# A fused attention and feed-forward kernel: in the first pair of blocks, flags, small products, weight loads and one operand's rounding are placed anew

## The chip, the core and the metric

The kernel runs on one core of one Trainium2 chip. The metric is the device time of one execution in microseconds (us), the median of several runs. TensorE (PE in the profile) does the matrix products, VectorE (DVE) and ScalarE (ACT) work between PSUM and SBUF, GpSimd (POOL) works on SBUF alone here, and SyncE (SP) issues nearly all DMA transfers. The engines run their own instruction streams in order and wait for each other on semaphores.

## What is computed

Linear attention without a softmax, a layer norm, a gated feed-forward part with two hidden layers, and a second layer norm, over 4096 tokens of 256 features. The weights of the feed-forward part are ternary numbers (times 8) with a scale for each output.

```python
def attn(x, wq, wk, wv, wo):                    # x (1, 4096, 256), D = 64
    Q, K, V = x @ wq.T, x @ wk.T, x @ wv.T
    energy = einsum('bnd,bne->bde', K, V)
    context = einsum('bnd,bde->bne', Q, energy) * sqrt(3 / D)
    return context @ wo.T

def ffn(x, w1, s1, w2, s2, h1, t1, h2, t2, w3, s3):   # 256 -> 1024 -> 1024 -> 1024 -> 256
    lin = lambda x, w, s: (x @ w.T) * s
    h = silu(lin(x, w1, s1)) * lin(x, w2, s2)
    h = gelu(lin(h, h1, t1))
    h = gelu(lin(h, h2, t2))
    return lin(h, w3, s3)

x = layernorm(x + attn(x, ...))
x = layernorm(x + ffn(x, ...))
```

## The kernel before

**Tiles.** The tokens are eight blocks of 512, worked on as four pairs (p = 0 to 3). Activations stand feature by token. Each fp32 activation that TensorE multiplies is given in two fp32r parts: ScalarE rounds it (`hi`, L674), VectorE subtracts (`lo`, L944), and both parts are multiplied with the same weights.

**Hidden layers.** Each of the two 1024x1024 layers of a pair is done by Winograd's form of the 2x2 product: seven products of 512x512 weights with 512x512 activations. I write product l.n for product n of hidden layer l (of the first pair, if nothing else is said). A product is four tiles j of eight matmuls (L1322), 32 in all, into four PSUM banks. GpSimd makes the differences of the activations (L506, L516, L525, L528), ScalarE copies sums out of PSUM (`copy_out`, L690) and applies the gelu (L720), VectorE adds (`add_first` L951, `add_fourth` L957, `add_third` L963). `R` has three slots, so product n uses slot n mod 3; the weights come through a ring of three slots as well (`load_ring`, L333).

**The first pair is special.** Its weights arrive in it. Eight units of the hidden weights (`unit`, 1 MB each) are loaded, GpSimd makes their sums in place (`combine`, L446 to L452), they are stored to a DRAM tensor `combos`, and the ring is loaded from there; two of the seven weight sets need no sums and are copied from DRAM to DRAM (`relay_hidden`). Blocks 2 to 7 load their residual rows late, since the upper halves of their places in `xr` hold `beside4` and `beside5`, a part of the sums.

**Flags and looks.** The products may take the rounded weights only if the low bits of all weights are zero. ScalarE sums the low bits as the weights arrive (`bits`, L569), TensorE adds these over the partitions (`flag_sum(s)`, L1211), VectorE makes a number 0 or 1 of it (`flag_out(s)`, L866 and L868), and TensorE reads it into a register and branches (`load_flag(s)`, L1217 and L1230). There are seven such looks; what follows look s in TensorE's stream can't start before the branch. Look 1 stands ahead of the first gated layer `first_l1` (L1262), look 2 ahead of product 0.0, look 3 ahead of 0.2, look 4 ahead of 1.0, look 5 ahead of 1.2.

**Order.** Everything is in an order written by hand, in loops for each engine: `first_l1`, `hidden`, and the list of transfers on SyncE. In `first_l1` ScalarE makes a silu (L640) and VectorE a gated product (`gate`, L938) for each of 8 chunks of two blocks (beta 0, 1); four PSUM banks are reused in turn, so tile t waits for the silu or the gate of tile t-4. All transfers of SyncE go through one queue in the order of issue, and a wait in that list holds all that stands behind it.

## Time and profile before

| | us |
|---|---|
| median of 3 runs | 653.07 (652.75 to 653.48) |
| the profiled execution, device time | 653.65 |
| its span in the trace | 651.9 |
| TensorE busy in the span | 637.2 (98%) |
| VectorE, ScalarE, GpSimd busy | 485.7, 410.7, 282.1 |

The profiled execution lies 0.58 us over the median, and 1.75 us of it lie outside the span. The granted clock of TensorE is at its upper level (1.00 of 2.4 GHz) in all slices of the span but the idle ends. In rows of a timeline the first number is the start in us, the second the time to the end of the last instruction of the row, then engine, line, operation, result and operands and a count, and in brackets the idle time of the engine ahead of it and who ended it. Ends of matmuls are modelled.

### The profile page before, as it was taken

To read this page: it belongs to the slowest core of one execution; us is meant where nothing else is said; L and a number is where in the kernel's file an instruction comes from. 1 tells how busy PE (TensorE), PEld (TensorE's weight loads), DVE (VectorE), ACT (ScalarE), POOL (GpSimd) and SP (SyncE) were. 2 spreads that over 40 slices of the span, in tenths; PEclk is the share of its full clock that TensorE was granted. 3 is DMA by queue.
4 is the path that set the end of the run, shared out by engine and by line. 5 is a ranking of instruction groups with operands and counts; after the bars stand their busy time and mean duration, and the time that the engine had idled before them with its cause. 6 is when DMAs were issued, how large, how long until landed. Compare 5 with 4: busy or idle time off the path is not lost.

```text
span 651.9 us, 9251 instructions
## 1 busy us (share of the span) xinstructions
PE 637.2 (98%) x3191; PEld 534.6 (82%) x3191; DVE 485.7 (75%) x717; ACT 410.7 (63%) x696; POOL 282.1 (43%) x226
## 2 busy tenths in 40 slices
PE   8989999999999999999999999999999999999995
PEld 6867788878889888888889888888889888888885
DVE  4677598789664997798655898698754899488476
ACT  5488789658761666557662657656763457666554
POOL 0367999295000663097000565079000367068034
PEclk9999999999999999999999999999999999999999
DMA  8989999764320036633330035734330015444201
GB/s 327 394 325 341 372 380 348 285 255 164 130 67 1 1 118 220 211 130 130 130 129 1 1 97 167 250 126 168 130 129 2 1 28 188 173 135 160 94 1 66
DMA packets 24370, 103.89 MB, mean 159 GB/s; under 512 B 2224, under 2 KB 3312, under 8 KB 16496
## 3 DMA queue, kind: packets, MB, share of 16 engines
q1 hardware_dynamic: 24032, 102.98, 44.5%
q8 instruction: 29, 0.48, 0.3%
q10 hardware_dynamic: 288, 0.26, 0.1%
q14 instruction: 21, 0.17, 0.1%
HBM read 87.51 MB, written 23.07 MB: 170 GB/s over the span
## 4 chain that ended last, share of the span: by engine, by line
PE 72%; DVE 3%; POOL 1%; issue 1%; ACT 1%; POOLq 0%; DVEq 0%; ACTq 0%
PE ps L1322 49%; PE ps L1262 13%; PE ps L1376 8%; DVE R L944 1%; DVE xr L928 1%; PE ps L1194 1%; PE ps L1182 1%; PE ps L1399 0%; ACT R L674 0%; DVE U L963 0%; POOL rstd L488 0%; POOL quarter L516 0%; ACT quarter L720 0%; POOL rstd L459 0%; POOL quarter L525 0%
## 5 line engine op out<-in xcount | busy, mean ns | idle before, releaser
L1322 PE MATMUL ps<-R,ring 128*128 128x512 f32 x1792 | 410.1, 390 | 1.6 <-DVE fsum L866 1.2
L1322 PEld LDWEIGHTS ps<-R,ring 128*128 128x128 f32 x1792 | 335.2, 188 | 71.6 <-DVE fsum L866 1.6
L944 DVE TENSOR_TENSOR R<-quarter,R 128x512 fp32r<-128x512 f32 x284 | 261.8, 944 | 62.6 <-ACT R L674 62.2
L674 ACT CAST R<-quarter 128x512 fp32r<-128x512 f32 x288 | 175.4, 616 | 30.6 <-POOL quarter L516 12.6
L1262 PE MATMUL ps<-x1T,w 128*128 128x512 f32 x512 | 119.4, 391 | 1.9 <-ACT sg L640 1.1
L720 ACT ACTIVATE quarter<-U,sc 128x512 f32<-128x512 f32 x96 | 69.5, 724 | 74.2 <-DVE U L963 29.4
L1262 PEld LDWEIGHTS ps<-x1T,w 128*128 128x128 f32 x512 | 95.2, 188 | 23.8 <-ACT sg L640 2.7
L506 POOL TENSOR_TENSOR quarter<-quarter,quarter 128x512 f32<-128x512 f32 x32 | 49.6, 1550 | 97.8 <-ACT quarter L720 91.1
L457 POOL TENSOR_TENSOR ve<-mv,eps 128x4 f32<-128x4 f32 x14 | 5.7, 404 | 181.5 <-DVE mv L921 181.5
L640 ACT ACTIVATE sg<-ps,sc 128x512 f32<-128x512 f32 x64 | 44.0, 689 | 61.3 <-PE ps L1262 61.1
L690 ACT COPY U<-ps 128x512 f32<-128x512 f32 x96 | 56.3, 586 | 31.3 <-PE ps L1322 31.3
L938 DVE SCALAR_TENSOR_TENSOR quarter<-ps,sc,sg 128x512 f32<-128x512 f32 x64 | 47.8, 746 | 23.7 <-ACT sg L640 13.4
L516 POOL TENSOR_TENSOR quarter<-quarter,quarter 128x512 f32<-128x512 f32 x32 | 48.9, 1527 | 16.7 <-DVE quarter L938 12.9
L1376 PEld LDWEIGHTS ps<-w,R 128*128 128x128 f32 x448 | 54.7, 192 | 0.7 <-DVE R L944 0.2
L1376 PE MATMUL ps<-w,R 128*128 128x256 f32 x448 | 55.1, 283 | 0.0
L528 POOL TENSOR_TENSOR quarter<-quarter,quarter 128x512 f32<-128x512 f32 x32 | 50.0, 1594 | 0.0
L525 POOL TENSOR_TENSOR quarter<-quarter,quarter 128x512 f32<-128x512 f32 x32 | 48.8, 1554 | 0.0
L928 DVE TENSOR_SCALAR xr<-xr,mv,rstd 128x256 f32<-128x256 f32 x52 | 35.5, 743 | 4.2 <-POOL rstd L459 4.2
L957 DVE TENSOR_TENSOR U<-ps,U 128x512 f32<-128x512 f32 x32 | 22.0, 690 | 14.7 <-PE ps L1322 14.7
L720 ACT ACTIVATE quarter<-ps,sc 128x512 f32<-128x512 f32 x32 | 22.1, 691 | 12.6 <-PE ps L1322 12.6
L963 DVE TENSOR_TENSOR U<-ps,U 128x512 f32<-128x512 f32 x32 | 21.8, 685 | 8.2 <-PE ps L1322 8.2
L446 POOL TENSOR_TENSOR beside<-unit 128x512 f32<-128x512 f32 x8 | 12.2, 1530 | 29.8 <-ACT junk L569 27.7
(84 smaller groups left out, 383.4 us busy)
## 6 DMA issues: line engine op xcount, KB each, us to landing
ring<-combos SPq DMA_DIRECT2D x56, 1024.0 KB, 4.9
combos<-unit SPq DMA_DIRECT2D x8, 1024.0 KB, 7.1
unit<-in_h1T SPq DMA_DIRECT2D x4, 1024.0 KB, 13.9
xr<-in_x_rows SPq DMA_DIRECT2D x8, 512.0 KB, 6.2
unit<-in_h2T SPq DMA_DIRECT2D x4, 1024.0 KB, 12.7
xT<-in_xT SPq DMA_DIRECT2D x7, 512.0 KB, 8.6
out<-xr SPq DMA_DIRECT2D x7, 512.0 KB, 2.9
w<-w_dram SPq DMA_DIRECT2D x3, 1024.0 KB, 7.5
```

Source lines behind the costliest of these rows:

```text
L506: nc.gpsimd.tensor_tensor(x12[:, c, :], x12[:, c, :], x11[:, c, :], ALU.subtract).then_inc(t_done, 1)
L516: nc.gpsimd.tensor_tensor(t2[:, c, :], x22[:, c, :], x12[:, c, :], ALU.subtract).then_inc(t_done, 1)
L525: nc.gpsimd.tensor_tensor(x11[:, c, :], t2[:, c, :], x11[:, c, :], ALU.subtract).then_inc(t_done, 1)
L528: nc.gpsimd.tensor_tensor(x21[:, c, :], x21[:, c, :], t2[:, c, :], ALU.subtract).then_inc(t_done, 1)
L674: nc.scalar.copy(R[slot_of(p, u)][:, 0, c, :], quarter[operand_home(p, u)][:, c, :]).then_inc(hi_done, 1)
L690: nc.scalar.copy(U[:, 1 if i == 2 else 0, j, :], ps[:, B + j, :]).then_inc(cp_done, 1)
L720: nc.scalar.activation(quarter[dst][:, j, :], src, ACT.Gelu, scale=sc[:, 2 + l, chunk:chunk + 1]).then_inc(gelu_done, 1)
L938: nc.vector.scalar_tensor_tensor(quarter[dst][:, j % KH, :], ps[:, base + (2 * j + 1) % 4, :], sc[:, 1, j:j + 1], sg[:, j % 2, :], ALU.mul ...
L944: nc.vector.tensor_tensor(r[:, 1, c, :], quarter[operand_home(p, u)][:, c, :], r[:, 0, c, :].bitcast(f32), ALU.subtract).then_inc(lo_done, 1)
L1262: last = nc.tensor.matmul(ps[:, base + t % 4, :], w, view(x1T[beta % 2][:, part, c, :]), start=n == 0, stop=n == 2 * EC - 1)
L1322: last = nc.tensor.matmul(ps[:, bank + j, :], w, view(R[slot_of(p, u)][:, part, k, :]), start=n in (0, 1, 5) and k == 0 and part == 0, sto ...
L1376: last = nc.tensor.matmul(rows_of(b)[:, q, :], view(slot[:, part, k, q * P:(q + 1) * P]), w, start=first and k == 0 and part == 0 and q % ...
```

## The change

- TensorE, front: `flag_sum(1)` moves ahead of the first transposes, and look 1 now stands between the second and the third of block 0's four transposed tiles (with it two of the projection products and the two halves of block 1's attention are behind the branch). VectorE makes flag 1 between the statistics and the last two normalised tiles.
- `first_l1`: ScalarE no longer rounds product 0.1's operand (`hi(0, 1, j)`) nor blocks 2 and 3's queries; VectorE makes both parts of that operand (`both_parts`: a copy that rounds, and the difference), after gates 1, 3, 5 and 7 of block 1. `flag_out(2)` stands behind the third of them. The sums of low bits (`bits_of_sums`) are cut in two pieces and spread, `bits_of_whole(4)` is one chunk later, `bits_of_whole(3)` one earlier.
- Hidden layer 0: the queries' two parts are made after the first four copies (ScalarE) and between the first sums (VectorE). `bits_of_sums` 5, 6, 7 are each one place later, 7 now ahead of layer 1. The attention of blocks 2 and 3 (L1182, sixteen matmuls) stood behind product 0.5; it is now behind tile 2 and behind tile 3 of it. `flag_sum(4)` moves from product 0.6 to behind tile 1 of 0.5, `flag_out(4)` from behind all of VectorE's layer work up to ahead of the fourth sums, and the residual additions of the two blocks stand two sums later (first) and behind the loop (second).
- SyncE: the two transfers of each `relay_hidden` are parted, the store of unit 3 and rings 1 and 2 go ahead of the loads of units 5 and 6, rings 3 and 4 and the rows of block 3 stand otherwise. `beside5` lies in other memory (that of `s3b`), so block 3's rows need not wait for unit 5, and the load of `s3b` moves from the start to the load of w3.

```diff
@@ memory
-            ... rows_at = [xr_at + 4096 * b + 2048 for b in (2, 3)]
-        beside_at = (c11_at, c11_at + 2048, c11_at + 4096, c11_at + 6144, *rows_at, sg_at + 2048, sg_at)
+        rows_at = xr_at + 4096 * 2 + 2048
+        beside_at = (c11_at, c11_at + 2048, c11_at + 4096, c11_at + 6144, rows_at, beside5_at, sg_at + 2048, sg_at)
@@ SyncE
             def load_rows_late(b):
                 sp.wait_ge(qlo_done, b + 1)
-                sp.wait_ge(unit_out[b + 2], UNIT_STORED)
-                sp.wait_ge(bits_done, n_bits("sums", b + 2))
+                if b == 2:
+                    sp.wait_ge(unit_out[4], UNIT_STORED)
+                    sp.wait_ge(bits_done, n_bits("sums", 4))
                 load_rows(b)
...
-            relay_hidden(0)
+            relay_hidden(0, 0)
             load_unit(4)
             store_unit(2)
             load_ring(0)
+            relay_hidden(0, 1)
+            store_unit(3)
             load_ring(1)
+            load_ring(2)
             load_unit(5)
-            store_unit(3)
             load_unit(6)
-            load_ring(2)
+            load_ring(3)
             load_unit(7)
             store_unit(4)
-            load_ring(3)
-            relay_hidden(1)
             load_ring(4)
+            relay_hidden(1, 0)
+            load_rows_late(3)
             load_rows_late(2)
+            relay_hidden(1, 1)
             load_ring(5)
             store_unit(5)
             load_ring(6)
             store_unit(6)
             load_ring(7)
-            load_rows_late(3)
             store_unit(7)
@@ ScalarE, hidden
+                if L == 1:
+                    bits_of_sums(7)
                 for j in range(KH):
                     copy_out(L, 0, j)
                     hi(p, u0 + 2, j)
                 if L == 0:
+                    hi_of_q(2)
+                    hi_of_q(3)
                     bits_of_whole(5)
...
@@ ScalarE, first_l1
             for j in range(HC):
                 silu(1, j, A)
-                if j == 0:
-                    bits_of_sums(1)
-                if j < KH:
-                    hi(0, 1, j)
-                if j == 1:
+                if j <= 1:
+                    bits_of_sums(1, range(j, j + 1))
+                if j == 2:
                     bits_of_whole(4)
-                if j == 4:
-                    bits_of_sums(2)
+                if 3 <= j <= 4:
+                    bits_of_sums(2, range(j - 3, j - 2))
@@ VectorE
+            def both_parts(c):
+                r, x = R[slot_of(0, 1)], quarter[operand_home(0, 1)]
+                dve.wait_ge(hi_done, n_split(0, 0, KH - 1))
+                dve.wait_ge(h_made, KH + c + 1)
+                nc.vector.tensor_copy(r[:, 0, c, :], x[:, c, :]).then_inc(hi_done, 1)
+                lo(0, 1, c)
...
-            normalised_tilewise(0, 0, attention_residual)
-            flag_out(1)
+            normalised_tilewise(0, 0, attention_residual, lambda: flag_out(1))
...
                 gate(0, 1, j, A)
                 if j == 0:
                     lo(0, 0, KH - 1)
-                elif j <= KH:
-                    lo(0, 1, j - 1)
+                elif j % 2 == 1:
+                    both_parts(j // 2)
                 if j == 5:
                     flag_out(2)
@@ VectorE, hidden
+                if L == 0:
+                    flag_out(4)
                 for j in range(KH + 1):
                     if j < KH:
                         add_fourth(L, j)
-                    if L == 0 and j == 1:
+                    if L == 0 and j == KH - 1:
                         residual1(a, B)
-                    if L == 0 and j == KH - 1:
-                        residual1(b, B + 2)
                     if j > 0:
                         lo(p, u0 + 7, j - 1)
+                if L == 0:
+                    residual1(b, B + 2)
...
-                if L == 0:
-                    flag_out(4)
@@ TensorE, hidden
+                def first_side(j):
+                    if j == 1:
+                        pe.wait_ge(gelu_done, n_gelu(0, 1, KH - 1))
+                        flag_sum(4)
+                    if j >= 2:
+                        if j == KH - 1:
+                            pe.wait_ge(fsum_done, 5)
+                        attention(j - 2)
+
+                product(p, l, 5, view, first_side if L == 0 else None)
```

TensorE around look 1, before: `x1T0` is the transposed block 0, `qs1` block 1's queries, and the rows run from the last projections to the first gated layer.

```order
L1194 MATMUL ps<-ident_72,xr_62 128x128 x2
L1145 MATMUL ps<-xhi3_112,wqr_100 128x512 x2
L1194 MATMUL ps<-ident_72,xr_62 128x128 x2
L1145 MATMUL ps<-xlo7_120,wqr_100 128x512 x2
L1211 MATMUL ps<-lowf_86,ones_73 1x4
L1194 MATMUL ps<-ident_72,xr_62 128x128 x2
L1182 MATMUL ps<-T1s_69,qs1_66 128x256 x4
L1194 MATMUL ps<-ident_72,xr_62 128x128 x2
L1182 MATMUL ps<-T1s_69,qs1_66 128x256 x4
L1217 TENSOR_LOAD flag_88
L1217 ISA x2
L1230 COMPARE_AND_BRANCH
```

The same place on TensorE after the change.

```order
L1224 MATMUL ps<-lowf_87,ones_74 1x4
L1207 MATMUL ps<-ident_73,xr_62 128x128 x2
L1158 MATMUL ps<-xhi3_113,wqr_101 128x512 x2
L1207 MATMUL ps<-ident_73,xr_62 128x128 x2
L1230 TENSOR_LOAD flag_89
L1230 ISA x2
L1243 COMPARE_AND_BRANCH
L1207 MATMUL ps<-ident_73,xr_62 128x128 x2
L1158 MATMUL ps<-xlo7_121,wqr_101 128x512 x2
L1207 MATMUL ps<-ident_73,xr_62 128x128 x2
L1195 MATMUL ps<-T1s_69,qs1_66 128x256 x8
```

The load and the branch moved from behind all twelve small matmuls to between them; two of four transposed tiles are now behind the branch.

VectorE in block 1's gates, before, from gate 2 to flag 2 (`R1` is product 0.1's operand, made from `quarter1`).

```order
L944 TENSOR_TENSOR R1_60<-quarter1_53,R1_60 128x512
L938 SCALAR_TENSOR_TENSOR quarter2_54<-ps,sc_71,sg_67 128x512
L944 TENSOR_TENSOR R1_60<-quarter1_53,R1_60 128x512
L938 SCALAR_TENSOR_TENSOR quarter3_55<-ps,sc_71,sg_67 128x512
L944 TENSOR_TENSOR R1_60<-quarter1_53,R1_60 128x512
L938 SCALAR_TENSOR_TENSOR quarter3_55<-ps,sc_71,sg_67 128x512
L866 TENSOR_REDUCE fsum_87<-ps 1x1
L868 TENSOR_SCALAR flag_88<-fsum_87 1x1
```

The same place on VectorE after the change.

```order
L958 CAST R1_60<-quarter1_53 128x512
L950 TENSOR_TENSOR R1_60<-quarter1_53,R1_60 128x512
L944 SCALAR_TENSOR_TENSOR quarter2_54<-ps,sc_72,sg_67 128x512 x2
L958 CAST R1_60<-quarter1_53 128x512
L950 TENSOR_TENSOR R1_60<-quarter1_53,R1_60 128x512
L944 SCALAR_TENSOR_TENSOR quarter3_55<-ps,sc_72,sg_67 128x512 x2
L958 CAST R1_60<-quarter1_53 128x512
L950 TENSOR_TENSOR R1_60<-quarter1_53,R1_60 128x512
L870 TENSOR_REDUCE fsum_88<-ps 1x1
L872 TENSOR_SCALAR flag_89<-fsum_88 1x1
```

Before, nothing but gate 5 stands right ahead of flag 2; now a copy and a difference do.

VectorE from the fourth sums (`add_fourth`, L957) to the first two third sums (L963) of layer 0, before.

```order
L957 TENSOR_TENSOR U_58<-ps,U_58 128x512 x2
L891 TENSOR_TENSOR xr_62<-ps,xr_62 128x1024
L944 TENSOR_TENSOR R1_60<-quarter5_57,R1_60 128x512
L957 TENSOR_TENSOR U_58<-ps,U_58 128x512
L944 TENSOR_TENSOR R1_60<-quarter5_57,R1_60 128x512
L957 TENSOR_TENSOR U_58<-ps,U_58 128x512
L891 TENSOR_TENSOR xr_62<-ps,xr_62 128x1024
L944 TENSOR_TENSOR R1_60<-quarter5_57,R1_60 128x512 x2
L866 TENSOR_REDUCE fsum_87<-ps 1x1
L868 TENSOR_SCALAR flag_88<-fsum_87 1x1
L963 TENSOR_TENSOR U_58<-ps,U_58 128x512 x2
```

And after the change.

```order
L870 TENSOR_REDUCE fsum_88<-ps 1x1
L872 TENSOR_SCALAR flag_89<-fsum_88 1x1
L971 TENSOR_TENSOR U_58<-ps,U_58 128x512 x2
L950 TENSOR_TENSOR R1_60<-quarter5_57,R1_60 128x512
L971 TENSOR_TENSOR U_58<-ps,U_58 128x512
L950 TENSOR_TENSOR R1_60<-quarter5_57,R1_60 128x512
L971 TENSOR_TENSOR U_58<-ps,U_58 128x512
L895 TENSOR_TENSOR xr_62<-ps,xr_62 128x1024
L950 TENSOR_TENSOR R1_60<-quarter5_57,R1_60 128x512 x2
L895 TENSOR_TENSOR xr_62<-ps,xr_62 128x1024
L977 TENSOR_TENSOR U_58<-ps,U_58 128x512 x2
```

The flag moved ahead of the sums, and both residual additions (L891, now L895) moved behind all four fourth sums.

## Rows read from the trace of the kernel before

**Rows 1.** The page's first part, busy time by engine (us, share, instructions).

```profile
PE 637.2 (98%) x3191; PEld 534.6 (82%) x3191; DVE 485.7 (75%) x717; ACT 410.7 (63%) x696; POOL 282.1 (43%) x226
```

**Rows 2.** Who TensorE waited for in the whole span (total us, times, longest).

```profile
PE ps L1194 <- ACT xr L631: 1.4, 1, 1.4
...
PE ps L1322 <- DVE fsum L866: 1.2, 1, 1.2
PE ps L1262 <- ACT sg L640: 1.1, 1, 1.1
PE ps L1262 <- ACT x1T L625: 0.7, 1, 0.7
...
PE ps L1322 <- issue: 0.4, 1, 0.4
```

**Rows 3.** Timeline of TensorE, 38 to 80 us.

```profile
38.79 0.44 PE L1194 MATMUL ps<-ident,xr 128*128 128x128 f32 x2
...
41.08 9.53 PE L1262 MATMUL ps<-x1T,w 128*128 128x512 f32 x40 [0.68 <-ACT x1T L625]
...
65.55 4.85 PE L1262 MATMUL ps<-x1T,w 128*128 128x512 f32 x20 [1.08 <-ACT sg L640]
...
73.86 5.72 PE L1322 MATMUL ps<-R,ring 128*128 128x512 f32 x24 [0.39 <-issue]
```

**Rows 4.** Timeline of VectorE, 39 to 72 us.

```profile
39.31 0.14 DVE L868 TENSOR_SCALAR flag<-fsum 1x1 int32<-1x1 f32 x1
...
59.54 1.12 DVE L944 TENSOR_TENSOR R<-quarter,R 128x512 fp32r<-128x512 f32 x1
...
63.01 0.72 DVE L944 TENSOR_TENSOR R<-quarter,R 128x512 fp32r<-128x512 f32 x1
...
71.79 0.14 DVE L868 TENSOR_SCALAR flag<-fsum 1x1 int32<-1x1 f32 x1
```

**Rows 5.** Timeline of GpSimd, 58 to 72 us.

```profile
58.48 1.63 POOL L448 TENSOR_TENSOR unit<-unit 128x512 f32<-128x512 f32 x1
...
65.06 1.29 POOL L446 TENSOR_TENSOR beside<-unit 128x512 f32<-128x512 f32 x1 [1.88 <-ACT junk L569]
...
71.43 1.29 POOL L506 TENSOR_TENSOR quarter<-quarter,quarter 128x512 f32<-128x512 f32 x1
```

**Rows 6.** Timeline of ScalarE, 58 to 65 us.

```profile
58.47 1.90 ACT L569 ACTIVATE junk<-unit 128x2048 uint8<-128x2048 uint16 x1
...
63.77 1.06 ACT L569 ACTIVATE junk<-unit 128x1024 uint8<-128x1024 uint16 x1 [0.95 <-DMA unit<-in_h2T]
...
64.83 0.67 ACT L640 ACTIVATE sg<-ps,sc 128x512 f32<-128x512 f32 x1
```

**Rows 7.** Busy time in two short stretches: engines, PEclk, DMA share, GB/s.

```profile
71.90:73.20 1.30, 1.30 (x7) 0.94 (x6) 0.72 (x2) 0.60 (x2) 1.17 (x2) 1.00 1.04 408
125.90:126.30 0.40, 0.40 (x4) 0.31 (x3) 0.40 (x1) 0.40 (x1) 0.00 (x0) 1.00 0.05 20
```

**Rows 8.** Timeline of TensorE, 117 to 160 us.

```profile
117.85 2.08 PE L1182 MATMUL ps<-T1s,qs 128*128 128x256 f32 x16
...
141.76 16.62 PE L1322 MATMUL ps<-R,ring 128*128 128x512 f32 x72 [1.16 <-DVE fsum L866]
...
159.42 1.06 PE L1194 MATMUL ps<-ident,xr 128*128 128x128 f32 x8 [0.17 <-DVE xr L928]
```

**Rows 9.** Timeline of VectorE, 119 to 158 us.

```profile
119.00 1.23 DVE L891 TENSOR_TENSOR xr<-ps,xr 128x1024 f32<-128x1024 f32 x1 [2.78 <-PE ps L1182]
...
125.81 1.29 DVE L963 TENSOR_TENSOR U<-ps,U 128x512 f32<-128x512 f32 x2
...
137.71 3.92 DVE L944 TENSOR_TENSOR R<-quarter,R 128x512 fp32r<-128x512 f32 x4
...
151.26 4.31 DVE L928 TENSOR_SCALAR xr<-xr,mv,rstd 128x256 f32<-128x256 f32 x4
...
157.90 1.38 DVE L928 TENSOR_SCALAR xr<-xr,mv,rstd 128x256 f32<-128x256 f32 x4
```

**Rows 10.** Timeline of GpSimd, 127 to 140 us.

```profile
127.41 1.29 POOL L506 TENSOR_TENSOR quarter<-quarter,quarter 128x512 f32<-128x512 f32 x1 [11.22 <-ACT quarter L720]
...
138.32 1.57 POOL L516 TENSOR_TENSOR quarter<-quarter,quarter 128x512 f32<-128x512 f32 x1
```

**Rows 11.** Timeline of SyncE's queue near 97 us, and that ring load's issue to landing.

```profile
97.76 0.43 SPq L333 DMA_DIRECT2D ring<-combos  x1
...
ring<-combos SPq DMA_DIRECT2D x1, 1024.0 KB, 8.6
```

More of the change, by code:

```diff
@@ L980, in hidden @@
                         add_first(L, j)
+                    if L == 0 and j < 2:
+                        lo_of_q(a + j)
                     if j > 0:
@@ L1345, in with_sums, with attention @@
                 product(p, l, 4, view)
[L1346 to L1350 removed]
+                def attention(i):
+                    pe.wait_ge(gelu_done, n_gelu(L, 1, 2 * i + 1))
+                    attention_out(a + i, lambda q, at=B + 2 * i: ps[:, at + q // 2, q % 2 * E:(q % 2 + 1) * E])
+                def first_side(j):
[7 more added lines that the diff above has]
+                product(p, l, 5, view, first_side if L == 0 else None)
+                if l == 0 and more and p > 0:
+                    attention(0)
+                    attention(1)
                 if p == 0 and l == 1:
```

74 lines of the change are left out of this document (33 added, 41 removed).

## The prediction, made before the changed kernel ran

> **What bounds the kernel.** I read the busy times first: TensorE is busy 637.2 of 651.9 us, no other engine over 75% [rows 1]. So the time can only change where TensorE waits, or where it gets more or less to do. Then the waits of TensorE: its largest are one of 1.4 us for the first normalised tile and one of 1.2 us for a flag's sum [rows 2]; its timeline shows the others of the first pair in brackets: 0.68 and 1.08 us in `first_l1`, 0.39 us ahead of product 0.0 [rows 3], 0.17 us between transposes at 159.42 us [rows 8]. Together this is under 5 us. Behind 183 us nothing is changed, and TensorE is held up there for under 1 us in all, so what the first pair gains or loses passes to the end one for one. A matmul of 512 columns takes 0.23 us (16.62 us for 72 in [rows 8]), a tile of four 0.91, a tile of eight 1.83, a product 7.3 us; these set the pace below.
>
> The profiled execution lay 0.58 us over the median. All terms are differences in it, and I take them from the median, 653.07 us.
>
> **Term 1, look 1.** Before, flag 1 is written at 39.45 us and the first gated matmul comes at 41.08, 1.63 us later [rows 3, 4]. At look 2 the distance is 1.93 us (71.93 to 73.86) [rows 3, 4]. This is what a look costs from flag to first matmul when DMA is full (share 1.04 there); at look 4 the stretch behind the flag has a DMA share of 0.05 [rows 7], and no wait is seen behind it. Now flag 1 is made behind the last aggregate, which ends at 37.7 us [rows 4], so by 38.0. The two tiles that are transposed behind the branch start at 38.0 + 1.63 = 39.6 us instead of 38.79 [rows 3]. DMA is as full there, so I take the full price. Two projections and a transposed tile follow, then ScalarE's and VectorE's parts of x1T, and the gated layer starts 0.8 us later. Bounds: 0.3 us, if the register load is quick, and 1.1 us, by the distance of look 2. The 1.4 us wait ahead of the first transpose stays: nothing that makes the first tile moved, and the flag's sum hides in it. **+0.8 us at this place**, but see term 3.
>
> **Term 2, ScalarE in the gated layer.** ScalarE waits 0.95 us for unit 4, sums its bits (1.06 us), and comes late to silu 2 of block 1 [rows 6]; TensorE waits 1.08 us for it at 65.55 [rows 3], with 0.15 us lost two tiles earlier, and 0.1 us to start anew: 1.3 us. Now four roundings (0.6 us each) and two query roundings are gone from ScalarE there, the long sum of 1.9 us is parted, and unit 4 is behind one transfer of 1 MB less and is looked at one chunk later. ScalarE then is back for every silu inside the 2 us that four banks allow. **-1.3 us**, hidden by term 3.
>
> **Term 3, flag 2.** Terms 1 and 2 only count if look 2 allows it, and VectorE's row decides that. With both, tile 7 of block 1 ends at 65.0 us and tile 11 at 68.6 (before, tile 8 began at 65.55; less 1.3, plus 0.8, is 65.0). GpSimd starts on unit 4 when ScalarE's look at it ends, at 64.2 now against 65.06, and from then works without a gap through 71.43 and beyond [rows 5]. VectorE and GpSimd hold each other up in SBUF: a difference that began at 59.54 took 1.12 us, since GpSimd's operation of 58.48 ran until 60.11 [rows 4, 5]; four normalising passes over 256 columns take 4.31 us at 151.26, where GpSimd works, and 1.38 us at 157.90, where it doesn't [rows 9]. So a copy with its difference costs between 1.1 us (0.5 and 0.6, alone) and 3.4 us (each held for an operation of up to 1.63 us [rows 5]). From gate 3: 65.0 + 0.8 = 65.8; copy and difference in the midst of GpSimd's row, 3.1: 68.9; gates 4 and 5, 0.7 each: 70.3; copy and difference, 1.9 if the copy comes ahead of GpSimd's next operation and 3.5 if behind: 72.2 to 73.8; reduce and compare 0.3: flag 2 at 72.5 to 74.1, middle 73.3, against 71.93 before. With 1.93 us for the look, product 0.0 starts at 75.2 us, against 73.86. **+1.3 us**, in place of terms 1 and 2. Bounds: if the copies don't get in GpSimd's way, gate 5 waits for tile 11 until 68.6, flag 2 is at 70.8, the product at 72.7: -1.1 us. If each of the four is held for a whole operation and the look costs 0.3 us more: 76.5, +2.6 us. I take the middle, since both kinds of operation are nearest to rows that show the holding.
>
> The Trainium skill speaks against this edit: GPSIMD Engine Reference, "Key points", says that GpSimd shares its SBUF interfaces with VectorE and contends with VectorE's instructions that read two SBUF inputs or run in a two-port mode. [rows 4, 5, 9] agree for the difference and the normalising pass; no row has a copy from SBUF. VectorE: DVE Perf Modes, "The perf-mode tier table", lists an fp32 copy inside SBUF at twice the rate of a two-input operation, which is such a mode. By the page the copy would thus be short but held like the others; if that were wrong, the sum would be the one of rival A.
>
> **Term 4, flag 5.** Before, TensorE waits at 141.76 for flag 5's sum to be read; the 24 matmuls ahead started at 134.86 and end by 140.4, so 1.4 us are lost [rows 8]. The chain back: VectorE's four differences (137.71, 3.92 us) [rows 9] wait for GpSimd's row of eight operations, from 127.41 to 139.9 [rows 10], which waits for the first gelu behind the third sums, and those start late, at 125.81, because VectorE stood 2.78 us at 119.00 for the attention behind product 0.5, made both residuals, and then waited for flag 4 [rows 9]. Now the attention's first half is ready 2 us earlier, flag 4 is read before the fourth sums, and the sums come in this order, on TensorE's pace: fourth sums until 119.6, first residual 120.8, two differences 122.0, second residual 123.1, third sums from 123.1. That is 2.7 us earlier; ScalarE has bits of a unit (2.75 us) between, and GpSimd can start at 124.7. Its eight operations then end at 137.2 instead of 139.9, the four differences by 139.2 (the statistics, 3.5 us, lie ahead of them), flag 5 at 139.5. TensorE needs it at 140.4. **-1.4 us**; bounds 0 (the chain gains under 1.4 us) and -1.4. All of this moves with TensorE, so the 1.3 us of term 3 don't eat into the margin.
>
> **Term 5.** The same chain brings the normalised blocks 3 us earlier, so the wait at 159.42 (0.17, and 0.1 to start anew) goes [rows 8]: **-0.3 us**. Parting the attention's 2.08 us in two [rows 8] adds one more turn between kinds of matmul: **+0.1 us** (0 to 0.2).
>
> **Transfers.** `s3b` is needed only behind 183 us, and its absence at the start brings nothing TensorE waits for earlier. Ring 0.1 now stands behind unit 3's store, ring 0.2 likewise: both land by 80 us, needed at 81.6 and 88.8. Unit 5 lands near 81, ScalarE wants it at 84. Block 3's rows come 20 us earlier. No term.
>
> **Sum:** +1.3 - 1.4 - 0.3 + 0.1 = -0.3 us, 652.8 us.
>
> **Rivals.**
> A. *VectorE's copies don't meet GpSimd.* Then product 0.0 starts near 72.7: -1.1 - 1.4 - 0.3 + 0.1 = -2.7 us, 650.4 us. For it: no copy of this kind in the trace, and look 1 may be quick. Against: GpSimd's row without a gap [rows 5], and differences are held in any case. From about 72.2 us for flag 2 downwards the gain passes 1.3 us. Chance 0.3.
> B. *The transfers become the bound (slower).* SyncE stands at block 2's rows until ScalarE has summed unit 4's low bits; before, ring 0.5 went out right behind that, at 97.76, and landed 8.6 us later, at 106.4 [rows 11]. Now a relay of 1 MB stands between, and block 3's rows ahead: 3 and 1.5 us more give 110.9, and product 0.5 is due at 110.6 + 1.3. If the queue is 3 us slower than that, TensorE waits 2 us: 654.8 us. It decides from 111.9 us on. Against: the relays were in the queue ahead of ring 0.4 before. Chance 0.07.
> C. *The chain to flag 5 isn't shortened.* VectorE and GpSimd hold each other there too. The 1.4 us stay: 654.2 us; with term 3 at its upper bound 655.5. Chance 0.13, half of it slower by over 0.2%.
> The forecast has 0.5.
>
> **How the numbers follow.** 0.2% (1.3 us) is about what a measurement can tell from no change. The forecast's own range is term 3's 72.5 to 74.1 us, 0.8 us to either side: 652.0 to 653.6. Faster: A, and a little of the forecast's edge, 0.32. Slower: B, half of C, and what I overlook, 0.15. Within: 0.53. The range reaches from near A's value to near B's: 650.8 to 654.6.
>
> **What the profile will show.** Term 1: the third transposed tile at 39.6 us, a gap ahead of it. Term 2: no wait at ScalarE's silu. Term 3: flag 2 between 72.5 and 74.1, product 0.0 1.9 us behind it. Term 4: no wait for a flag's sum near 141 us, GpSimd's row starting some 2.7 us earlier against product 0.6. Term 5: none at the transposes. I am wrong if flag 2 comes by 71.5, if product 0.5 waits for its ring, or if the first gated layer starts no later than before.

## The result and the profile after

| | before | changed |
|---|---|---|
| median of 22 runs each, us | 652.88 (651.38 to 654.27) | 653.76 (652.48 to 655.57) |
| ratio | | 1.0016 [1.0010, 1.0022] |
| the profiled execution, us | 653.65 | 653.82 |

By the ratio, the changed kernel is 1.0 us slower (0.7 to 1.4), and by the two medians 0.9, where 0.3 us faster was forecast. It lies inside the range given and within 0.2%, but the sign was wrong.

TensorE's largest waits in the changed kernel, by who ended them (total us, times, longest):

```profile
PE ps L1332 <- issue: 1.9, 1, 1.9
...
PE ps L1207 <- DVE xr L1086: 1.1, 1, 1.1
PE ps L1207 <- ACT xr L637: 1.1, 1, 1.1
...
PE ps L1275 <- issue: 0.5, 1, 0.5
```

Against [rows 2] three waits are gone: for the flag's sum (1.2), for the silu (1.1) and for x1T (0.7). Two are new: 1.9 us ahead of product 0.0 (L1332) and 1.1 us at look 1 (L1207). TensorE's timeline of the changed kernel shows their places:

```profile
36.61 0.41 PE L1207 MATMUL ps<-ident,xr 128*128 128x128 f32 x2 [1.06 <-ACT xr L637]
...
39.24 0.43 PE L1207 MATMUL ps<-ident,xr 128*128 128x128 f32 x2 [1.14 <-DVE xr L1086]
...
42.45 9.52 PE L1275 MATMUL ps<-x1T,w 128*128 128x512 f32 x40
...
75.11 5.68 PE L1332 MATMUL ps<-R,ring 128*128 128x512 f32 x24 [1.94 <-issue]
...
117.60 1.11 PE L1195 MATMUL ps<-T1s,qs 128*128 128x256 f32 x8
...
120.39 1.11 PE L1195 MATMUL ps<-T1s,qs 128*128 128x256 f32 x8
...
136.10 22.07 PE L1332 MATMUL ps<-R,ring 128*128 128x512 f32 x96
158.00 1.91 PE L1207 MATMUL ps<-ident,xr 128*128 128x128 f32 x16
```

The row at 39.24 us is the third of block 0's transposed tiles, the first matmul behind look 1. The gated layer starts at 42.45 us (41.08 in [rows 3]) and product 0.0 at 75.11 (73.86). Later the row from 136.10 runs 22 us without a break, over the place of the 1.16 us wait of [rows 8], and the transposes are one row of sixteen. So the tail gains about what the head loses, and the two traces end alike: 652.0 and 651.9 us of span. That is not the whole result, since the medians differ by more; and one thing in the changed trace was in no row of before. These are short stretches of it: length, busy time of TensorE, weight loads, VectorE, ScalarE and GpSimd, then the granted clock as a share of 2.4 GHz, the DMA share and GB/s.

```profile
39.48:42.89 3.41, 3.41 (x16) 3.02 (x15) 1.28 (x3) 1.56 (x3) 3.25 (x3) 0.51 0.51 196
...
43.00:46.00 3.00, 3.00 (x15) 2.44 (x14) 2.17 (x4) 2.06 (x4) 1.27 (x1) 1.00 0.27 101
```

For 3.4 us behind the wait at look 1, TensorE's clock stands at its lower level, 1.2 GHz, and then at 2.4 GHz again.

### The profile page after: what moved, and what is told of

It reads as the page before. It is cut to its first block, busy times and chain, and to the rows that moved or that the text cites. A ratio compares the mean times of both kernels' runs of the same rounds, so it can differ in the third digit from the quotient of the medians.

```text
span 652.0 us, 9260 instructions
## 1 busy us (share of the span) xinstructions
PE 637.9 (98%) x3191; PEld 536.5 (82%) x3191; DVE 494.9 (76%) x721; ACT 408.4 (63%) x692; POOL 282.1 (43%) x226
## 4 chain that ended last, share of the span: by engine, by line
PE 93%; DVE 3%; issue 2%; POOL 1%; DMA 1%; ACT 1%; SPq 0%; POOLq 0%; DVEq 0%; ACTq 0%
PE ps L1332 61%; PE ps L1275 17%; PE ps L1401 8%; PE ps L1175 2%; PE ps L1195 1%; PE ps L1158 1%; PE ps L1207 1%; DMA xT<-in_xT 1%; POOL rstd L494 1%; PE ps L1183 1%; DVE R L950 1%; DVE U L977 0%; PE ps L1424 0%; ACT quarter L728 0%; DVE quarter L944 0%
## 5 line engine op out<-in xcount | busy, mean ns | idle before, releaser
L1332 PE MATMUL ps<-R,ring 128*128 128x512 f32 x1792 | 409.9, 390 | 1.9 <-issue 1.9
L1332 PEld LDWEIGHTS ps<-R,ring 128*128 128x128 f32 x1792 | 335.2, 188 | 71.5 <-issue 2.3
L682 ACT CAST R<-quarter 128x512 fp32r<-128x512 f32 x284 | 173.0, 616 | 27.5 <-POOL quarter L534 9.9
L934 DVE TENSOR_SCALAR xr<-xr,mv,rstd 128x256 f32<-128x256 f32 x52 | 35.5, 743 | 4.2 <-POOL rstd L465 4.2
L905 DVE TENSOR_TENSOR U<-ps,s3b 128x1024 f32<-128x1024 f32 x7 | 8.5, 1219 | 21.6 <-PE ps L1401 21.6
```

The lines of the kernel that those rows point to most:

```text
L682: nc.scalar.copy(R[slot_of(p, u)][:, 0, c, :], quarter[operand_home(p, u)][:, c, :]).then_inc(hi_done, 1)
L1332: last = nc.tensor.matmul(ps[:, bank + j, :], w, view(R[slot_of(p, u)][:, part, k, :]), start=n in (0, 1, 5) and k == 0 and part == 0, sto ...
```

## The experiments

Each kernel ran beside the kernel before on the same chip; ratios are to that. The diffs are against the changed kernel or the kernel before, as said. e1 to e4 ran on one chip, e5 to e8 on a second and e9 to e12 on a third; the kernel before measured 652.73, 652.97 and 652.59 us there (29, 26 and 17 runs).

### Four edits of the changed kernel: which of the new waits matters

**e1, look 1 as before** (flag 1's sum, its making, and the look with the small matmuls).

```diff
@@ TensorE
                 q_pieces(range(23, 28), view)
-                pe.wait_ge(tile_sum[0], 1)
-                flag_sum(1)
                 ...
                 transposed_first(1)
+                q_pieces(range(30, 32), view)
+                pe.wait_ge(tile_sum[0], 1)
+                flag_sum(1)
+                transposed_first(2)
+                attention_half(0)
+                transposed_first(3).then_inc(tr_ready, 1)
+                attention_half(1).then_inc(op_ready, 1)
@@ VectorE
-            normalised_tilewise(0, 0, attention_residual, lambda: flag_out(1))
+            normalised_tilewise(0, 0, attention_residual)
+            flag_out(1)
```

> The changed kernel with look 1, flag 1's sum and flag 1's making where they stood before. Theory C (the clock): in the profile of the changed kernel TensorE's granted clock is 0.50 from 39.5 to 42.9 us, right behind the 1.1 us gap at look 1, and the gated layer starts at 42.45 instead of 41.08 us. With look 1 back the clock stays at 1.00 there, the layer starts at 41.1, and the time is 1.0 to 2.0 us under the changed kernel's (ratio to before 0.9975 to 0.9995). Rival F (flag 2 decides): product 0.0 waits for VectorE's flag 2 anyway, so an earlier layer brings under 0.5 us (ratio 1.0008 to 1.0020).

Measured: 653.68 us (651.61 to 654.61), ratio 1.0009 [1.0000, 1.0018]. Its traced execution is a short one (650.2 us of span) with no low clock; product 0.0 comes at 73.59 us, still behind a wait of 2.0 us. The ratio is in the range of rival F and not in that of theory C: look 1 alone doesn't explain the median. The traced execution is the second shortest of eleven. The runs' mean clocks part them: six at 0.994, median 653.85 us, and five at 0.997, median 652.32; what a mean clock says of a run is worked out further down.

**e2, the look behind all small matmuls**, with flag 1's sum and making early as in the change.

```diff
                 transposed_first(1)
+                transposed_first(2)
+                q_pieces(range(30, 32), view)
+                transposed_first(3).then_inc(tr_ready, 1)
+                attention_half(0)
+                attention_half(1).then_inc(op_ready, 1)
```

> The changed kernel with flag 1 summed and made early, as changed, but the look put behind all of the small products, ahead of the gated layer. Theory C: no gap, no fall of the clock, the layer starts at 40.9 to 41.1 us, time as in the run with look 1 undone or up to 0.2 us less. Rival F: within 0.5 us of the changed kernel.

Measured: 653.59 us (652.09 to 654.13), ratio 1.0012 [1.0003, 1.0020]. The wait for the third transposed tile is gone, yet the clock is at its lower level again:

```profile
37.51 0.41 PE L1207 MATMUL ps<-ident,xr 128*128 128x128 f32 x2 [1.05 <-ACT xr L637]
...
39.16 0.56 PE L1207 MATMUL ps<-ident,xr 128*128 128x128 f32 x2
```

```profile
39.34:42.75 3.41, 3.41 (x15) 3.07 (x15) 1.51 (x3) 2.24 (x6) 3.06 (x4) 0.50 0.66 255
```

So the fall at look 1 doesn't need the wait there. The last wait of TensorE over 0.3 us ahead of it is the one of 1.05 us for the first transposed tile, which ended 1.8 us earlier, and the kernel before has a wait of 1.4 us in that place and no low clock behind it. What e2 shares with the changed kernel, and e1 and before don't have, is flag 1's sum ahead of the first tile instead of among the others. Which of the two makes the clock fall there, this early sum or the wait, no run separates. The low clock by itself costs 1.1 us here: the gated layer starts 4.99 us behind the first transposed tile, and 3.92 in e1. Nine of the eleven runs have a mean clock of 0.996 or less. The median is within 0.5 us of the changed kernel's, as rival F had it.

**e3, filling the wait at look 1** with six matmuls over zeros.

```diff
                 transposed_first(1)
+                keep_clock(6, 1)
```

> The changed kernel with six bf16 matmuls on zeros (0.21 us each, into a bank that nobody reads) in TensorE's queue ahead of look 1, so that TensorE works while the sequencer waits for the register. Theory C: the look's delay stays (third transposed tile at 39.2 us or little later), the clock stays at 1.00, the layer starts at 41.7 to 41.9 instead of 42.45, and the time is 0.3 to 0.7 us under the changed kernel's, with less spread between runs. If the clock only followed the work and cost nothing, the time is that of the changed kernel.

Measured: 655.73 us (653.25 to 656.30), ratio 1.0039 [1.0025, 1.0053]: worse, so the expectation fell. In the trace the clock stays up at look 1, but behind the wait ahead of product 0.0 it is down, and the first 24 matmuls of product 0.0 take 7.31 us where the changed kernel's trace has 5.68:

```profile
75.07 7.31 PE L1332 MATMUL ps<-R,ring 128*128 128x512 f32 x24 [1.92 <-issue]
```

```profile
75.38:78.80 3.42, 3.42 (x10) 2.65 (x9) 2.88 (x3) 0.46 (x3) 3.29 (x3) 0.50 0.98 389
```

Another 1.0 us is lost at 186.39 us, five matmuls behind a branch, ended by nothing that the profile shows; its cause is open. The two runs with a mean clock of 0.999 took 653.25 and 655.01 us, so the low clock isn't all of the loss either.

**e4, flag 2 ahead of the third copy and difference.**

```diff
-                elif j % 2 == 1:
+                elif j % 2 == 1 and j != 5:
                     both_parts(j // 2)
                 if j == 5:
                     flag_out(2)
+                    both_parts(2)
```

> The changed kernel with flag 2 made right behind gate 5, ahead of the third copy and difference on VectorE. In the changed kernel flag 2 comes at 74.06 us, product 0.0 at 75.11, behind a gap of 1.94 us. Theory F: flag 2 at 70.9 to 71.2, product 0.0 at 73.2 (the layer's own end) to 73.4, the time 1.5 to 1.9 us under the changed kernel's (ratio to before 0.9985 to 0.9997). Theory C alone, in which the first layer's start decides: no change, since the gain at flag 2 would turn into another wait ahead of product 0.0.

Measured: 651.56 us (651.17 to 652.70), ratio 0.9984 [0.9975, 0.9993]. One flag's place turns the change from slower into faster: flag 2 is written at 70.22 us instead of 74.06, product 0.0 starts at 72.24 with no wait over 0.2 us, and the trace has no low clock.

```profile
72.24 5.60 PE L1333 MATMUL ps<-R,ring 128*128 128x512 f32 x24
```

So the wait ahead of product 0.0 decides the sign. Not all low clock is gone, since look 1 is still as in the change: four of the eleven runs have a mean clock of 0.994 or 0.995 (median 652.13 us), the other seven 0.997 or more (651.42).

### Four kernels on the clock

The mean granted clock of each timed run says whether it had such a stretch: 3.41 us at half the clock take 0.0026 off the mean over 652 us. The idle end of a span counts too: in the fourteen traces the clock is at its lower level over the last 1.0 to 4.4 us, when TensorE has nothing left to do, which takes off 0.0008 to 0.0034. So a run without a stretch lies between 0.9966 and 0.9992, and the groups' borders aren't sharp. The changed kernel's runs fall into groups (32 runs: the 22 of the result, which suggested the theory, and ten of e8): 7 runs with 0.997 or more, median 652.77 us (652.13 to 654.44); 17 with 0.994 to 0.996, 653.81 (653.01 to 654.47); 8 with 0.992, 654.97 (654.49 to 655.57). The 72 such runs of the kernel before, over all the experiments, have 0.997 or more but for two, and a median of 652.80.

**e5, flag 2 early and look 1 as before**: e4's and e1's edits together.

> The changed kernel with look 1, flag 1's sum and flag 1's making where they stood before, and with flag 2 made ahead of VectorE's third copy and difference of product 0.1's operand. Theory S (the clock): the changed kernel has two longer waits of TensorE in the first pair, 1.1 us at look 1 (39.24 us) and 1.9 us ahead of product 0.0 (75.11 us); behind either, in a part of the runs, the granted clock lies at 0.50 for 3.41 us (seen from 39.48 us in the changed kernel, from 75.4 us in the one with six filling matmuls, 3), which costs 1.3 to 1.6 us, and this is why the changed kernel's median lies 0.9 us over before's. Here both waits are gone: no run has a mean clock under 0.997, the runs lie within 1 us of each other, and the median is 651.2 us, 0.3 to 0.5 below the kernel with flag 2 early alone. Theory M (the waits alone, the clock being chance that meets all kernels alike): look 1 costs about 0.7 us whatever the clock does, so the median is 650.8 us, and some runs have a mean clock of 0.994 or 0.995 as before.

Measured: 650.96 us (650.59 to 651.23), ratio 0.9963 [0.9947, 0.9978]. No run is under 0.997, and all six lie within 0.7 us of each other. The median is between those of S and M; the clocks speak for S. Product 0.0 follows the gated layer without a wait:

```profile
68.94 3.02 PE L1277 MATMUL ps<-x1T,w 128*128 128x512 f32 x12
71.79 5.60 PE L1334 MATMUL ps<-R,ring 128*128 128x512 f32 x24
```

**e6, look 1 alone moved, in the kernel before** (e1's diff the other way round).

> The kernel before with one part of the change: flag 1's sum, flag 1's making and look 1 placed as in the changed kernel. Theory S: ahead of the third transposed tile TensorE now waits 1.0 to 1.2 us, and in 3 to 7 of ten runs the mean clock is 0.994 to 0.996, against 0.997 and more in all 29 runs of the kernel before. Look 1's later start (0.3 us without a lower clock, 1.4 us with it) is partly taken in by the 1.1 us wait for ScalarE at 65 us only if that is for unit 4, which does not move: so the median is 0 to 0.5 us over before's, and the runs with the low clock are not much slower. Theory M: the later start of the gated layer is hidden by that wait for unit 4: ratio 1.000, and no run has a lower clock than before's.

Measured: 653.34 us (652.86 to 655.13), ratio 1.0009 [0.9999, 1.0020]; 4 of 11 runs have 0.996 or less. The median is 0.4 us over before's, which can't be told from none. Its trace has the low stretch at look 1 and nowhere else:

```profile
39.25:42.66 3.41, 3.41 (x15) 3.02 (x14) 1.77 (x3) 1.56 (x3) 3.17 (x4) 0.50 0.93 356
```

The gated layer starts 5.53 us behind the first transposed tile (3.92 without the moved look), and yet flag 2 is written only 0.3 us later behind that tile than in both traces of the kernel before (35.5 and 35.2 us): the wait for ScalarE in block 1 takes most of the delay in, as expected, and product 0.0 follows flag 2 after 1.40 us instead of 1.93 and 1.84. The two runs with 0.994 and 0.996 are among the fastest (652.86 and 652.92 us), the two with 0.992 are the slowest (654.34 and 655.13).

**e7, flag 2 later, in the kernel before**, nothing else.

```diff
-                if j == 5:
+                if j == 7:
                     flag_out(2)
```

> The kernel before with flag 2 made behind gate 7 instead of gate 5 of block 1, nothing else. Flag 2 is then written near 74.6 us (71.93 before), and product 0.0 starts at 75.7 to 76.5 us by look prices of 1.05 and 1.93 us, so TensorE waits 2.2 to 3.0 us there, like the 1.94 us of the changed kernel. Nothing behind it takes the delay in. Theory S: in a good part of the runs the mean clock is 0.994 to 0.996, those runs are 1.6 us slower than the others, and the median is 2.5 to 4 us over before's (655.2 to 656.7 us). Theory M: no run's mean clock is under 0.997, and the median is 1.8 to 2.6 us over before's (654.5 to 655.3 us).

Measured: 655.80 us (654.27 to 657.00), ratio 1.0036 [1.0023, 1.0050]. This puts the changed kernel's wait into a kernel that has nothing else of the change, and the clock falls behind it:

```profile
75.89 7.25 PE L1322 MATMUL ps<-R,ring 128*128 128x512 f32 x24 [2.14 <-issue]
```

```profile
75.72:79.13 3.41, 3.24 (x8) 2.60 (x9) 0.00 (x0) 0.49 (x2) 3.21 (x3) 0.50 0.81 292
```

Three of eight runs have 0.996 or less, median 656.18 us; the other five 654.81. By these medians the wait itself costs 1.8 us (654.81 less before's 652.97), and the low stretch 1.4 more where it comes, but the groups are small and overlap (one run with 0.998 took 656.85 us). The whole median is in the range of S and above that of M. I expected a good part of the runs to have the stretch; three of eight bear that out only weakly, the trace shows it plainly.

**e8, the changed kernel again.**

> The changed kernel once more, unchanged, beside the others, for a second trace and for the spread of its mean clock. Theory S: the mean clocks fall in three groups, about 0.997, 0.995 and 0.992 (none, one and two stretches of 3.41 us at 0.50), with medians about 652.7, 653.8 and 654.9 us, and the runs in the first group are no slower than before's. If the trace has a low stretch, it begins within 1 us behind the wait at 39.2 us or the one at 75.1 us and nowhere else. Theory M: mean clocks and times are not ordered so, or a low stretch stands elsewhere.

Measured: 654.40 us (652.13 to 655.25), ratio 1.0015 [1.0004, 1.0026]. This trace has both stretches, one at each new wait:

```profile
38.40:41.85 3.45, 2.77 (x11) 2.48 (x12) 0.56 (x2) 1.41 (x5) 3.10 (x4) 0.51 0.80 308
75.98:79.40 3.42, 3.42 (x10) 2.65 (x9) 2.65 (x3) 1.10 (x2) 3.29 (x4) 0.50 1.01 411
79.40:82.80 3.40, 3.40 (x16) 2.53 (x16) 1.65 (x2) 1.68 (x4) 3.27 (x3) 1.00 0.55 227
```

Ten matmuls in 3.42 us, then sixteen in 3.40. Its execution has a mean clock of 0.992, the lowest group. The stretches begin 0.6 us ahead of the first wait's end and 1.1 us behind the second's, so a little outside the places that I had given. Of these ten runs alone, the test of the theory, two have 0.997 or more, five 0.994 to 0.996 (median 654.12 us) and three 0.992 (654.96). The one with 0.998 took 652.13 us; the other, with 0.997, took 654.44, so the clock is not all that varies, and that the first group is no slower than before's can't be told from two runs. The two lower groups and both places of the stretches are as the theory of the clock (S) had them, and the theory of waits alone (M) falls.

### Four kernels on the terms

**e9, the part in hidden layer 0 alone, in the kernel before**: the attention between the tiles of product 0.5, flag 4 early, the residual additions later.

```diff
@@ VectorE
+                if L == 0:
+                    flag_out(4)
                 for j in range(KH + 1):
                     ...
-                    if L == 0 and j == 1:
-                        residual1(a, B)
                     if L == 0 and j == KH - 1:
-                        residual1(b, B + 2)
+                        residual1(a, B)
                     ...
+                if L == 0:
+                    residual1(b, B + 2)
                 ...
-                if L == 0:
-                    flag_out(4)
@@ TensorE
-                product(p, l, 5, view)
+                product(p, l, 5, view, first_side if L == 0 else None)
```

> The kernel before with one part of the change, in hidden layer 0: the attention of blocks 2 and 3 behind tiles 2 and 3 of product 0.5, flag 4's sum behind tile 1 of it, flag 4 made ahead of the fourth sums, the two residual additions later. All of the gated layer, look 1, flag 2, ScalarE's and SyncE's order stay as before. If terms 4 and 5 of the prediction hold by themselves, TensorE's wait for flag 5's sum near 141 us (1.16 us) and the one at the transposes (0.17 us) are gone, no run has a mean clock under 0.996, and the median lies 1.3 to 1.7 us under before's (651.2 to 651.6 us). Rival: the earlier chain also needs the bits' sums that the change moved on ScalarE, so flag 5 is only 0 to 0.7 us earlier and the median lies 0 to 0.8 us under before's.

Measured: 650.89 us (650.15 to 652.37), ratio 0.9969 [0.9958, 0.9980], no run under 0.997. Both waits of the tail are gone with the head as before:

```profile
134.83 22.06 PE L1319 MATMUL ps<-R,ring 128*128 128x512 f32 x96
156.74 1.91 PE L1194 MATMUL ps<-ident,xr 128*128 128x128 f32 x16
```

This part by itself is worth 1.7 us by the medians (2.0 by the ratio, 1.3 to 2.7), and the rival that needs ScalarE's new order for it falls.

**e10, the rounding back on ScalarE**, look 1 as before.

```diff
@@ ScalarE, block 1
                 silu(1, j, A)
+                if j < KH:
+                    hi(0, 1, j)
@@ VectorE
-                elif j % 2 == 1:
-                    both_parts(j // 2)
+                elif j <= KH:
+                    lo(0, 1, j - 1)
```

> The changed kernel with look 1 as before and with the rounding of product 0.1's operand back on ScalarE (VectorE makes its differences behind gates 1 to 4, as before); flag 2 behind gate 5. Theory H (VectorE's copies, held up by GpSimd, make flag 2 late, and the 1.9 us wait lowers the clock): VectorE writes flag 2 1.0 to 1.8 us sooner than in the kernel with look 1 undone alone (72.54 us there, first transposed tile at 36.63), so 70.7 to 71.5; TensorE waits about 1 us for ScalarE in block 1 again and 0 to 0.4 us ahead of product 0.0, no run has a mean clock under 0.996, and the median is 651.0 to 651.8 us. Rival (flag 2 is late by ScalarE's other order, the parted sums of low bits): flag 2 stays within 0.5 us of 72.5, and the median stays near 653.

Measured: 651.18 us (650.54 to 652.34), ratio 0.9978 [0.9969, 0.9987], no run under 0.997. VectorE's row ahead of flag 2:

```profile
69.04 0.72 DVE L952 TENSOR_TENSOR R<-quarter,R 128x512 fp32r<-128x512 f32 x1
69.69 0.74 DVE L946 SCALAR_TENSOR_TENSOR quarter<-ps,sc,sg 128x512 f32<-128x512 f32 x1
70.35 0.14 DVE L872 TENSOR_REDUCE fsum<-ps 1x1 f32<-1x4 f32 x1
70.52 0.14 DVE L874 TENSOR_SCALAR flag<-fsum 1x1 int32<-1x1 f32 x1
```

Flag 2 comes at 70.66 us instead of 72.54 in e1, 1.9 us sooner. TensorE waits 0.6 us for ScalarE (not 1.0) and not ahead of product 0.0. So VectorE's copies make flag 2 late, and not ScalarE's parted sums, which this kernel keeps.

**e11, ScalarE's look at unit 4's low bits later**, look 1 as before: GpSimd stands idle while VectorE makes the second and most of the third pair of parts.

```diff
-                if j == 2:
-                    bits_of_whole(4)
-                if 3 <= j <= 4:
-                    bits_of_sums(2, range(j - 3, j - 2))
+                if j == 5:
+                    bits_of_whole(4)
+                if 6 <= j <= 7:
+                    bits_of_sums(2, range(j - 6, j - 5))
```

> The changed kernel with look 1 as before and with ScalarE's look at unit 4's low bits behind silu 5 of block 1 instead of silu 2 (the sums of unit 2 behind it), so that GpSimd starts on unit 4 some 4 to 5 us later and stands idle while VectorE makes the second and third pair of parts of product 0.1's operand. Theory H: the second and third copy take 0.42 us as the first does (1.40 and 1.45 us in the kernel with look 1 undone alone), the differences 0.69 (1.67), flag 2 comes at 70.8 us instead of 72.54, and product 0.0 starts at 71.9 to 72.2 instead of 73.59. Rival (the copies are slow for another reason, such as ScalarE reading the same memory): copies and differences stay over 1.2 us, and flag 2 stays near 72.5. What GpSimd does later may hold something else up, so the whole time is open: 650.5 to 656 us.

Measured: 656.24 us (655.70 to 656.77). First VectorE, then GpSimd, of this kernel:

```profile
65.32 0.42 DVE L958 CAST R<-quarter 128x512 fp32r<-128x512 f32 x1
65.77 0.69 DVE L950 TENSOR_TENSOR R<-quarter,R 128x512 fp32r<-128x512 f32 x1
...
68.95 0.42 DVE L958 CAST R<-quarter 128x512 fp32r<-128x512 f32 x1
69.40 1.67 DVE L950 TENSOR_TENSOR R<-quarter,R 128x512 fp32r<-128x512 f32 x1
```

```profile
69.17 1.35 POOL L452 TENSOR_TENSOR beside<-unit 128x512 f32<-128x512 f32 x1 [7.00 <-ACT junk L575]
```

The same two places in the changed kernel, VectorE and then GpSimd:

```profile
66.35 1.39 DVE L958 CAST R<-quarter 128x512 fp32r<-128x512 f32 x1
67.77 1.67 DVE L950 TENSOR_TENSOR R<-quarter,R 128x512 fp32r<-128x512 f32 x1
...
70.68 1.45 DVE L958 CAST R<-quarter 128x512 fp32r<-128x512 f32 x1
72.16 1.66 DVE L950 TENSOR_TENSOR R<-quarter,R 128x512 fp32r<-128x512 f32 x1
...
73.92 0.14 DVE L872 TENSOR_SCALAR flag<-fsum 1x1 int32<-1x1 f32 x1
```

```profile
66.16 1.29 POOL L454 TENSOR_TENSOR unit<-unit 128x512 f32<-128x512 f32 x1
67.53 1.36 POOL L456 TENSOR_TENSOR unit<-unit 128x512 f32<-128x512 f32 x1
```

A copy takes 0.42 us with GpSimd idle and 1.39 or 1.45 beside it; a difference 0.69 and 1.67. The last difference of e11 meets GpSimd's first operation, which began 0.2 us ahead of it, and takes the 1.67 again. Flag 2 is at 71.31 us (70.8 was expected: the one held difference), product 0.0 at 72.37. The Trainium skill says in SBUF — State Buffer, "Who interferes with whom", that GpSimd and VectorE take turns at a shared pair of ports, for whole instructions, and that whoever issues first gets it; these rows agree. The whole kernel is slow for another reason: TensorE waits 2.97 us at 98.06 us for a copy of ScalarE's, again with a low clock behind it. GpSimd's differences of the activations start at 75.00 us here and at 69.02 in e1, and I take the wait to come from that; it wasn't tried.

```profile
98.33:101.70 3.37, 3.37 (x9) 2.61 (x9) 3.37 (x3) 3.37 (x6) 3.37 (x3) 0.50 0.08 30
```

**e12, the kernel before again.**

> The kernel before, unchanged, for a second trace of it. In the first, two places of the head were slower than in the kernels above that have the same code there: the first gated layer began 4.31 us behind the first transposed tile (3.91 to 3.92 in the two others with look 1 as before), and product 0.0 came 1.93 us behind flag 2, with a register load of 1.17 us (1.40 us and 0.65 us in the kernel with only look 1 moved). If these are the profiled execution's own, the second trace has about 3.9 and 1.1 to 1.5 us there, and a span of 650.8 to 651.3 us instead of 651.9. If they belong to the kernel, both come again.

Measured: 654.03 us, one execution, span 652.2. The expectation that both slow places would go held for one of them. The gated layer starts 3.92 us behind the first transposed tile (3.91 to 3.93 in e1, e5, e7, e9 and e10 as well), so the 4.31 of the first trace (36.77 to 41.08) was that execution's own. The slow look 2 came again: a register load of 1.12 us, and product 0.0 1.84 us behind flag 2. And this traced execution too lies over the kernel's median, by 1.4 us (0.8 in the first). The two traces of before are thus of executions longer than its median, which is why the changed kernel's trace, at its own median, seemed to lose only 0.17 us. What makes before's runs spread over 2.5 us with the clock up is open. A part may lie ahead of look 1: the first transposed tile starts between 36.21 and 37.51 us in the fourteen traces.

## Why the prediction was wrong, term by term

**Term 1, look 1: right in kind, too small.** The price of 1.63 us was read at a place where the row itself says that TensorE waited for ScalarE's x1T [rows 3], not for the look; here it took 1.51 us from flag 1 to the third transposed tile. That tile was due at 39.6 and came at 39.24; the gated layer was due 0.8 us later and came 1.37 later in the trace. In e4, with the clock up, it starts 4.39 us behind the first transposed tile, against 3.92 with look 1 as before: 0.5 us. With a low stretch it is 5.5 to 5.8 us (e6, e8, the changed kernel). So the look costs 0.5 us, within the bounds of 0.3 to 1.1, and the clock another 1.1 to 1.5, which the sum didn't have.

**Term 2, ScalarE: right.** There is no wait for the silu at 65 us.

**Term 3, flag 2: its sum came out right (+1.25 for +1.3) by luck, since errors cancel.** Flag 2 was put at 73.3 us and came at 74.06, the end of the range. Some 0.6 us of this is the layer's late start with the low clock (gate 3 ended at 66.4 us and not at 65.8), and 0.4 that both operations behind gate 5 were held, where I had taken the middle; for the pair behind gate 3 I had 3.1 us, and it took 3.1. In e3, where the clock stays up at look 1, product 0.0 starts 37.56 us behind the first transposed tile, against 38.50 in the changed kernel and 37.09 in the kernel before. So of the 1.4 us only about 0.5 are there without the low stretch. The other way, the look was priced at 1.93 us and took 1.05. The reason given for 1.93, that DMA is full, is wrong: e7 takes 1.05 us (74.84 to 75.89) with a DMA share of 1.04,

```profile
74.88:75.20 0.32, 0.00 (x0) 0.00 (x0) 0.00 (x0) 0.32 (x1) 0.32 (x1) 1.00 1.04 410
```

and the long register loads (1.17, 1.12 and 1.08 us in the first trace of before, e12 and e9) stand beside TensorE's last matmuls of the gated layer, but so does the 0.30 of e10. What makes one long is open. It isn't spread by chance over the kernels: in the nine traces with the changed kernel's order of transfers the load at look 2 takes 0.30 to 0.32 us, and of the five with the order of before four have 0.65 to 1.17 (e7, with its flag 3 us later, has 0.33). The new order may thus have made looks cheaper, which had no term in the sum; no run has it alone. So the range of term 3 held the start of product 0.0, and yet the term missed what follows from the wait: **a wait of 1.9 us ahead of product 0.0 lets the clock fall in a part of the executions**, and the next 24 matmuls then take 7.3 us instead of 5.7.

**Term 4, flag 5: right**, and e9 shows it alone. GpSimd's row starts at 126.32 us, 9.8 us ahead of the matmuls behind flag 5's sum (136.10); before, it was 127.41 [rows 10] against 134.86, 7.4 us: 2.3 us earlier by TensorE's pace (2.7 were forecast), and the wait is gone. **Term 5: right**, the transposes don't wait. Together with the parted attention, e9 measures 1.7 us for the 1.6 of the sum. **Transfers: right**; TensorE waits for no ring. The attention takes twice 1.11 us instead of once 2.08: 0.1 us more, as in the sum.

**The failed step** is thus the one that counted TensorE's waits at their own length and nothing more: the +0.8 us of look 1 and the +1.3 us ahead of product 0.0 held nothing for the clock behind them. The runs with a mean clock of 0.996 or less go by these two places:

| where TensorE meets a new or longer wait | kernels | runs with 0.996 or less |
|---|---|---|
| look 1 and product 0.0 | changed (with e8) | 25 of 32 |
| product 0.0 alone | e1, e7 | 6 of 11, 3 of 8 |
| look 1 alone | e4, e6 | 4 of 11, 4 of 11 |
| neither | before; e5, e9, e10 | 2 of 72; 0 of 24 |

(Not in the table: e2 with 9 of 11, e3 with 4 of 6 and e11 with 3 of 4. Each has a wait of 1.9 us or more, and an arrangement of its own around it or at look 1.)

Where the mean clock shows no low stretch, the changed kernel's median is 652.77 us, 0.1 below before's 652.88, where the forecast had 0.3 below. These are seven runs from 652.13 to 654.44 us, so the sign of that remainder isn't shown. Over all runs it is 653.76; 25 of the 32 runs have at least one low stretch by their mean clock, each worth about 1.1 us by the groups' medians; that is about 1.1 us on the mean of the runs, the size of the miss. [Rows 7] showed a clock of 1.00 in two short stretches and I took it for a constant of the kernel, though by my own sum the change put a wait ahead of product 0.0 that was well over the 0.39 us of before; it measured 1.94.

**Rivals.** A didn't happen: the copies are held (e11 shows what it would have been, flag 2 at 71.3). B didn't: nothing waits for a transfer. C didn't: e9. What did happen was none of them. I had a place, a price and a condition for each wait, and none for the clock. Open are what starts the fall at look 1 (e2), and what the new order of transfers does by itself.

The best kernels here are parts of the change: e9 (650.89 us), e5 (650.96) and e10 (651.18), 0.2 to 0.4% faster than before. They ran on two chips, and the runs don't tell them apart.

## What to carry to other kernels

Where a change trades short waits of TensorE for fewer and longer ones, even at an equal sum, look at the granted clock behind each wait and at the mean clock of every run, not of one trace, and know what the idle end of the span adds to it. When a step's result gates another engine (a flag, a branch), put it ahead of any work on its engine that another engine can hold up. And move parts of a change one at a time: here the part in the hidden layer was worth 1.7 us, and an earlier look 1 and a later flag 2 gave all of it back and more.

## What was not expected of the hardware

- Around a wait of 1.9 us (product 0.0), or two of 1.1 us with little work between (look 1), TensorE ran 3.4 us at 1.2 GHz, in some executions of one kernel and not in others. In seven such places the stretch began between 0.6 us ahead of the wait's end and 1.1 us behind it; in an eighth, e2, with no wait at look 1, it began 1.8 us behind the end of the last one. The kernel before waits 1.4 us ahead of its first transposed tile, and its traces show no low clock there.
- The same register load at look 2 took 0.30 to 1.17 us in the fourteen traces; neither the DMA share nor TensorE's work explains which, and the long ones are all in kernels with the transfers in the order of before.
- A copy of 128x512 from SBUF to SBUF goes from 0.42 to 1.45 us beside GpSimd, more than threefold, since it is held for the rest of GpSimd's operation and not slowed in proportion.
